# A recurrent attention layer and a top-2 expert layer on one core: the combination of expert outputs moved into the block loop

## The chip, the cores and the metric

The kernel runs on one core of one Trainium2 chip. The time is the device time of one execution in microseconds (us). Before the change it is 735.64 us, the median of three runs (734.95 to 736.15).

## The reference, cut to what matters

```python
# x: (2, 2048, 256)
x = layernorm(x + attn(x))       # token mixing, three 256x256 projections, an exponential
                                 # recurrence over T (wkv), a gate, an output projection
x = layernorm(x + ffn(x))
# ffn: 8 experts, 2 of them for each token
logits = x @ Wg + bg                                     # (tokens, 8)
topk_scores, topk_idx = top_k(logits, 2)
topk_scores = softmax(topk_scores)
comb = (one_hot(idx, 8) * topk_scores[..., None]).sum(axis=1)
h = einsum('td,edf->etf', tokens, W1) + b1[:, None, :]   # 256 -> 1024
a = where(even expert, gelu(h), silu(h))
y = einsum('etf,efd->etd', a, W2) + b2[:, None, :]       # 1024 -> 256
out = einsum('te,etd->td', comb, y)
# layernorm(z) = (z - mean) / sqrt(var + 1e-5)
```

## The kernel before, in words

All engines run programs of their own, and wait for each other by semaphores that are written out by hand. There are three stages.

The **chunk stage** walks over 8 chunks of 256 times 2 tokens (`chunks`, steps -2 to 9; a step works on several chunks at once). VectorE runs the scans of the recurrence (`stabilise`, `accumulate`, `numerator`, `divide`) and picks two experts for each token of an older chunk (`choose`, `place`). ScalarE runs, in each step and in this order, `exponents` (Relu and Exp, L1006 to L1011, whose result B is what `accumulate` multiplies at L1304), `bonuses` (Exp), `copy_x1T`, `gates` (Sigmoid), `upper_halves`, `inverse` (Ln and Exp), `normalise_x1` and `copy_v`. TensorE projects (`project_k` waits for VectorE's `nd`). GpSimd sends each token's normalised row, a record of 256 values and two numbers, to its two places in a table in DRAM, `records_dram`, sorted by expert (`send_records`, eight indirect DMAs a chunk); its spare time goes into splitting the weights of expert 0.

Every product of the experts is made from numbers that are split in an upper part (fp32r) and a lower part (the rest), in three products each. So weights and activations are split first.

The **block stage** works on blocks of 256 records of one expert. The count of blocks depends on the data, and tables made at its start (`row_t`, `ex_t`, `par_t`, `full_t`, VectorE's `link` chain) tell for each block where it lies, its expert, the slot of the weights and whether its second half holds anything. For a block t: ScalarE loads the records (`load_records`, three blocks ahead), TensorE transposes them (`turn_records`), VectorE splits the result (`halves`) and works out for each row where its output goes (`dest`, L1210), TensorE makes the first product (L897, 48 matmuls of 256 columns), ScalarE the function and the upper parts (L1102, L1108), VectorE the lower parts (L1220), TensorE the second product in two halves (L906, 24 matmuls each), VectorE adds the bias b2 (L1228, `outputs`), GpSimd scatters the rows to `expert_out_dram` with two indirect DMAs (L674). TensorE's order is: transposes of t+2, first product of t+1, second product of t. The code of TensorE is unrolled; VectorE, ScalarE and GpSimd run a loop with four blocks in its body (`blocks`). GpSimd also splits the weights of expert e (`split`, L580 and L584) when the blocks of expert e-2 are through; SP has loaded them as they are into one buffer (`staging`, 2 MB), one expert ahead. Two slots hold split weights (`wx`).

The **combination stage** begins when all rows have been written. SP loads for 16 pieces of 128 times 2 tokens the two expert rows of each token (`yy`; the rows x1 are there already), VectorE and ScalarE weigh them with the softmax scores and add x1, VectorE takes mean and variance, GpSimd a power of -0.5, ScalarE normalises, SP stores.

## Time and profile before

| | us |
|---|---|
| median of three runs | 735.64 |
| the profiled execution | 734.4 |
| its span, first to last instruction | 732.7 |
| TensorE busy | 643.3 (88%) |
| VectorE busy | 458.7 (63%) |
| ScalarE busy | 392.6 (54%) |
| GpSimd busy | 304.5 (42%) |
| TensorE in the chain that ended last | 72% |

In the profile PE is TensorE, PEld its weight loads, DVE VectorE, ACT ScalarE, POOL GpSimd and SP the sync engine. A name such as SPq is an engine's own instruction queue. L906 is line 906 of the kernel. Matmuls overlap, so their mean duration (283 ns) is more than the distance between two. The share of an engine over the span is a mean over three stages with different limits: the chunk stage lasts to about 250 us, the block stage to 672, the combination stage to the end. `[1.21 <-ACT ...]` behind an instruction is how long its engine stood idle ahead of it and what ended that.

### The profile page before, as it was taken

Reading aid. Unit: us, or ns where it says so; the run is one execution under the profiler, and the core shown is the slowest. Engines: PE = TensorE matmul, PEld = TensorE weight load, DVE = VectorE, ACT = ScalarE, POOL = GpSimd, SP = SyncE. Lnnn points to the kernel's source line nnn. Section 1 sums busy time; section 2 is a strip of 40 time slices with the busy share of each in tenths; the row PEclk is TensorE's granted clock in tenths of the full one; section 3 lists DMA queues with packets and bytes.
Section 4 is the critical chain, followed back from the end, with each engine's and each line's share of the span. In section 5 each row is a group of like instructions: output and inputs, shape, how many; then the busy total and the mean of one; then the engine's idle time right before and its main releaser. Section 6 shows DMA issues by size and latency. Waiting matters only on the chain.

```text
span 732.7 us, 14811 instructions
## 1 busy us (share of the span) xinstructions
PE 643.3 (88%) x4525; PEld 594.2 (81%) x4525; DVE 458.7 (63%) x963; ACT 392.6 (54%) x715; POOL 304.5 (42%) x353
## 2 busy tenths in 40 slices
PE   7999999999777889999999999999999999996000
PEld 4787877888655779999999999999999999996000
DVE  4879999999996465574654654455544543432694
ACT  3577577568742243654546363655645455551474
POOL 5111144654565636292361732551821821112363
PEclk9999999999987599999999999999999999999555
DMA  8400133132226517914141141141241121100893
GB/s 256 135 30 25 63 117 108 65 104 82 104 76 231 184 56 227 312 28 173 43 154 52 44 159 53 42 159 51 67 138 36 34 59 46 31 28 31 274 306 115
DMA packets 57116, 78.75 MB, mean 107 GB/s; under 512 B 5190, under 2 KB 46611, under 8 KB 56884
## 3 DMA queue, kind: packets, MB, share of 16 engines
q1 hardware_dynamic: 41540, 51.59, 21.8%
q0 software_dynamic: 6496, 16.99, 6.5%
q10 hardware_dynamic: 8976, 8.72, 4.4%
q8 instruction: 73, 1.20, 0.7%
q14 instruction: 31, 0.25, 0.1%
HBM read 49.14 MB, written 28.92 MB: 107 GB/s over the span
## 4 chain that ended last, share of the span: by engine, by line
PE 72%; DVE 10%; issue 7%; POOL 4%; ACT 3%; DMA 3%; SPq 0%; ACTq 0%; another core or an unknown queue 0%; DVEq 0%; POOLq 0%
PE hT_ps L897 28%; PE y_ps L906 26%; PE vr_ps L734 6%; PE k_ps L734 5%; PE xT_ps L915 2%; PE wo_ps L742 2%; POOL records_dram L639 2%; DVE o_all L1242 1%; PE xT_ps L725 1%; PE small_ps L756 1%; DMA yy<-expert_out_dram 1%; DMA recs<-records_dram 1%; POOL rstd_c L693 1%; PE xT_ps L804 1%; ACT res L1163 1%
## 5 line engine op out<-in xcount | busy, mean ns | idle before, releaser
L897 PE MATMUL hT_ps<-xTh,wx 128*128 128x256 f32 x1120 | 213.6, 288 | 3.8 <-DVE aTl L1220 2.6
L906 PE MATMUL y_ps<-wx,aTh 128*128 128x256 f32 x1088 | 197.5, 283 | 1.1 <-DVE y_sb L1228 1.1
L897 PEld LDWEIGHTS hT_ps<-xTh,wx 128*128 128x128 f32 x1120 | 179.9, 195 | 4.5 <-DVE aTl L1220 2.8
L1220 DVE TENSOR_TENSOR aTl<-hT_ps,aTh 128x512 fp32r<-128x512 f32 x140 | 93.1, 688 | 124.2 <-ACT aTh L1108 118.5
L906 PEld LDWEIGHTS y_ps<-wx,aTh 128*128 128x128 f32 x1088 | 169.7, 192 | 1.3 <-issue 1.3
L674 POOL DMA_INDIRECT expert_out_dram<-y_sb,dest x70 | 68.2, 975 | 238.3 <-DVE y_sb L1228 222.7
L897 PE MATMUL hT_ps<-xTl,wx 128*128 128x256 f32 x560 | 160.1, 286 | 0.0
L906 PE MATMUL y_ps<-wx,aTl 128*128 128x256 f32 x544 | 154.0, 283 | 0.0
L1102 ACT ACT_TABLE_LOAD x33 | 42.3, 1283 | 170.3 <-PE hT_ps L897 167.5
L1102 ACT ACTIVATE hT_ps<-hT_ps,b_c 128x256 f32<-128x256 f32 x280 | 113.3, 466 | 23.2 <-PE hT_ps L897 20.3
L897 PEld LDWEIGHTS hT_ps<-xTl,wx 128*128 128x128 f32 x560 | 109.1, 195 | 0.0
L906 PEld LDWEIGHTS y_ps<-wx,aTl 128*128 128x128 f32 x544 | 104.4, 192 | 0.0
L639 POOL DMA_INDIRECT records_dram<-rec,slot_i x64 | 75.3, 1177 | 65.8 <-DVE rec L1366 34.4
L734 PE MATMUL vr_ps<-xh,wq 128*128 128x512 f32 x256 | 86.6, 410 | 0.0
L1108 ACT ACTIVATE aTh<-hT_ps 128x512 fp32r<-128x512 f32 x140 | 83.8, 643 | 0.0
L1228 DVE TENSOR_TENSOR y_sb<-y_ps,b_b 128x256 f32<-128x256 f32 x70 | 29.4, 424 | 80.8 <-PE y_ps L906 79.0
L584 POOL TENSOR_TENSOR wx<-staging,wx 128x512 fp32r<-128x512 f32 x56 | 70.3, 1298 | 0.6
L734 PEld LDWEIGHTS vr_ps<-xh,wq 128*128 128x128 f32 x256 | 49.7, 194 | 11.8 <-ACT v L1001 0.3
L734 PE MATMUL vr_ps<-xl,wq 128*128 128x512 f32 x128 | 51.8, 405 | 0.0
L734 PE MATMUL k_ps<-xh,wq 128*128 128x512 f32 x128 | 42.2, 401 | 3.7 <-DVE nd L1249 2.7
L1210 DVE SCALAR_TENSOR_TENSOR dest<-recs,own_f 128x1 int32<-128x1 f32 x66 | 37.4, 607 | 0.1
L734 PEld LDWEIGHTS k_ps<-xh,wq 128*128 128x128 f32 x128 | 24.2, 189 | 10.3 <-issue 4.7
(201 smaller groups left out, 864.4 us busy)
## 6 DMA issues: line engine op xcount, KB each, us to landing
staging<-in_L_ffn_W SPq DMA_DIRECT2D x16, 1024.0 KB
recs<-records_dram ACTq DMA_DIRECT2D x33, 258.0 KB
yy<-expert_out_dram SPq DMA_DIRECT2D x16, 512.0 KB, 5.3
xin<-in_L_attn_x SPq DMA_DIRECT2D x16, 256.0 KB
xres<-in_L_attn_x SPq DMA_DIRECT2D x16, 256.0 KB, 3.1
x_dram<-rec SPq DMA_DIRECT2D x16, 256.0 KB
xx<-x_dram SPq DMA_DIRECT2D x2, 2048.0 KB
out<-res SPq DMA_DIRECT2D x16, 256.0 KB, 4.0
```

The costliest lines, as they stand in the source:

```text
L584: pool.tensor_tensor(wx[:, e % 2, 1, at], raw[:, at], wx[:, e % 2, 0, at].bitcast(F32), ALU.subtract).then_inc(weights_ready if n == LOWER ...
L639: pool.indirect_dma_start(xs, bass.IndirectOffsetOnAxis(ap=slot_i[at][:, n:n + 1], axis=0), rec[at][:, j, :], None, bounds_check=DUMMY - 1 ...
L674: pool.indirect_dma_start(ys, bass.IndirectOffsetOnAxis(ap=dest[t.slot][:, h:h + 1], axis=0), y_sb[t.slot][:, h, :], None, bounds_check=2 ...
L734: ins = pe.matmul(out_ps.rearrange("p (b t) -> p b t", b=B), wq[:, mat, now, part, cc, oc * P:(oc + 1) * P], xpart[c.slot][:, cc, :, now:n ...
L742: ins = pe.matmul(wo_bank(c, b)[:, h, :], mixed[:, cc, b, h * P:(h + 1) * P], wo[:, cc, :], start=cc == 0, stop=cc == CC - 1)
L897: ins = pe.matmul(hT_ps[b][:, f, :], wx[:, s, part, off:off + P], xpart[t.slot % 2][:, cc, :], start=k == 0, stop=k == len(terms) - 1)
L906: ins = pe.matmul(y_ps[h], apart[t.slot % 2][:, fc, h * P:(h + 1) * P], wx[:, s, part, off:off + C], start=k == 0, stop=k == len(terms) - 1)
L1102: act.activation(hT_ps[b][:, f, :], hT_ps[b][:, f, :], func, bias=b1_c[:, bass.ds(expert * FC + (2 * b + f), 1)]).then_inc(act_done, 1)
L1108: act.activation(aTh[u.slot % 2][:, 2 * b - 2:2 * b, :], hT_ps[b - 1][:], ACT.Copy).then_inc(aTh_done, 1)
L1210: dve.scalar_tensor_tensor(out=dest[u.slot][:, h:h + 1], in0=recs[u.slot][:, h, C + 1:REC], scalar=own[:, :, h:h + 1].rearrange("p a b -> ...
L1220: dve.tensor_tensor(aTl[u.slot % 2][:, 2 * b:2 * b + 2, :], hT_ps[b][:], aTh[u.slot % 2][:, 2 * b:2 * b + 2, :].bitcast(F32), ALU.subtract ...
L1228: dve.tensor_tensor(y_sb[u.slot][:, h, :], y_ps[h], b2_b[:, bass.ds(expert * C, C)], ALU.add).then_inc(y_done, 1)
```

## The change

The combination is done block by block. Since a layer norm doesn't change when its input is doubled and its epsilon multiplied by 4, the kernel works with 2z = (x1 + 2 g y) + (x1 + 2 g' y'), one bracket for each of a token's two experts. A record now holds 261 numbers: row, token, place of the first choice, the later one of its two places, and the two scores, which ScalarE makes in the chunk stage as sigmoids of the gap between the two logits (`weigh`). In the block stage:

- `mark`: eight small VectorE operations tell from the record whether this is the token's first or second visit, where it goes, and its weight.
- `share_half`: after the bias, a second VectorE operation makes x1 + 2 g y.
- GpSimd scatters the share to `x1_dram` where the visit is the token's first (`keep_shares`), gathers the earlier share for tokens on their second (`gather`), takes the power for the variances (`spread_z`) and scatters the finished rows to the output (`send_rows`): six indirect DMAs a block instead of two. Rows that are not concerned get an index out of bounds and are skipped.
- VectorE adds both shares and takes mean and variance (`add_other`, one block later), and normalises (`normalise`, two blocks later).

The combination stage, its loads and stores are gone. ScalarE no longer loads records; the sync engine does, and it fetches raw weights at the blocks that a new table names (`split_steps`, 13 operations once, at block 2). The split of weights leaves GpSimd: ScalarE writes the upper part in four pieces, VectorE the lower in four, behind `normalise`. The loops are unrolled on all engines. The core of the diff (declarations and the removed combination code left out):

```diff
-    LOWER = 8
+    SPLITS = 4
+    SECOND = EARLY + 1
+    MARKS = 8
     REGION = TOKENS + BLK
     DUMMY = E * REGION
-    REC = C + 2
+    REC = C + 5
...
+            def load_records(u):
+                row = sp.value_load(row_t[0:1, bass.ds(u.number, 1)], min_val=0, max_val=DUMMY)
+                sp.dma_start(recs[u.slot][:], xs[bass.ds(row, BLK), :].rearrange("(h p) c -> p h c", p=P)).then_inc(rec_in[u.slot], 16)
+
+            sp.wait_ge(pads_out, 16 * (E - 2))
+            for n in range(EARLY):
+                sp.wait_ge(share_done, early_block(n).upto(BH))
+                load_records(early_block(RING + n))
+            sp.wait_ge(weights_ready, 2)
+            load_raw(2)
+            sp.wait_ge(split_known, 1)
+
+            def block_step(t):
+
+                u = t + RING
+                if u.exists:
+                    with if_used(sp, used, u):
+                        sp.wait_ge(share_done, t.upto(BH))
+                        load_records(u)
+                fetch = sp.value_load(fetch_t[0:1, bass.ds(t.number, 1)], min_val=0, max_val=2)
+                with sp.If(fetch > 0):
+                    expert = sp.value_load(next_t[0:1, bass.ds(t.number, 1)], min_val=0, max_val=E - 3)
+                    sp.wait_ge(weights_ready, expert + 2)
+                    load_raw(expert + 2)
+
+            blocks_in_line(sp, used, 0, block_step)
...
+                          base=TC * c.number, channel_multiplier=1,
                           allow_small_or_imprecise_dtypes=True).then_inc(label_done, 1)
                 pool.wait_ge(label_done, c.upto(1))
+                pool.wait_ge(weighed, c.upto(2))
                 pool.wait_ge(x1_done, c.upto(J))
...
+            def spread_z(t):
+                pool.wait_ge(mv_z_done, since_second(t) * BH)
+                after(pool, row_done, since_second(t - RING) * BH)
+                pool.tensor_tensor(var_z[:], mv_z[t.slot][:, :, 1], eps4_b[:], ALU.add).then_inc(var_done, 1)
+                pool.wait_ge(var_done, since_second(t))
+                pool.tensor_tensor(rstd_z[t.slot][:], var_z[:], half_neg[:, 0:BH], ALU.pow).then_inc(rstd_z_done, 1)
+
+            def keep_shares(t):
+
+                pool.wait_ge(marks, t.upto(8))
+                pool.wait_ge(share_done, t.upto(BH))
+                take_wait(pool)
+                for h in range(BH):
+                    pool.indirect_dma_start(
+                        rows_1, bass.IndirectOffsetOnAxis(ap=where_to[t.number % MARKS][:, 0, h:h + 1], axis=0),
+                        share[t.slot][:, h, :], None, bounds_check=TOKENS - 1, oob_is_err=False).then_inc(share_out[t.slot], 16)
+
+            def gather(t):
+
+                pool.wait_ge(marks, t.upto(8))
+                pool.wait_ge(share_out[(t - 1).slot], (t - 1).turn(16 * BH, 16 * BH))
+                after(pool, sum_done, since_second(t - RING))
+                take_wait(pool)
+                for h in range(BH):
+                    pool.indirect_dma_start(
+                        other[t.slot][:, h, :], None, rows_1,
+                        bass.IndirectOffsetOnAxis(ap=where_to[t.number % MARKS][:, 1, h:h + 1], axis=0),
+                        bounds_check=TOKENS - 1, oob_is_err=False).then_inc(other_in[t.slot], 16)
+
+            def send_rows(t):
+                pool.wait_ge(row_done, since_second(t) * BH)
+                take_wait(pool)
+                for h in range(BH):
+                    pool.indirect_dma_start(
+                        rows_2, bass.IndirectOffsetOnAxis(ap=where_to[t.number % MARKS][:, 1, h:h + 1], axis=0),
+                        row_out[t.slot][:, h, :], None, bounds_check=TOKENS - 1, oob_is_err=False).then_inc(out_done[t.slot], 16)
+
+            keep_shares(early_block(0))
+
+            def block_step(t):
+                for stage, u in ((keep_shares, t - 1), (send_rows, t - 2), (gather, t), (spread_z, t - 1)):
+                    if stage is keep_shares:
+
+                        if t.exists:
+                            with if_used(pool, used, t, t.number - 1):
+                                stage(u)
+                    elif u.exists and with_second(u):
+                        with if_used(pool, used, u, t.number - 1):
+                            stage(u)
+
+            blocks_in_line(pool, used, 2, block_step)
...
+                pe.wait_ge(share_done, (t - 1).upto(BH, 1))
+                with pe.If(slot == 0):
+                    product2(t, 0, 0)
+                with pe.Else():
+                    product2(t, 1, 0)
+                pe.wait_ge(share_done, (t - 1).upto(BH))
+                with pe.If(full == 0):
+                    pe.sem_inc(mm2_done[1], 1)
+                with pe.Else():
...
+            def weigh(c):
+
+                at = c.number % RECS
+                act.wait_ge(gap_done, c.upto(1))
+                scattered(act, c)
+                act.activation(rec[at][:, :, C + 3], gap[:], ACT.Sigmoid, scale=-1.0).then_inc(weighed, 1)
+                act.activation(rec[at][:, :, C + 4], gap[:], ACT.Sigmoid).then_inc(weighed, 1)
...
+                if (i - 3).exists and i.number < NCH:
+                    weigh(i - 3)
                 if i.exists:
...
+                if i.number == NCH:
+                    weigh(i - 2)
                 if (i - 1).exists:
                     normalise_x1(i - 1)
+                if i.number in (NCH - 1, NCH + 1):
+                    weigh(i - 2)
                 if (i + 1).exists and i.number >= 0:
...
+            def split_upper(t):
+
+
+                kind = act.value_load(split_t[0:1, bass.ds(t.number, 1)], min_val=0, max_val=2)
+                with act.If(kind > 0):
+                    expert = act.value_load(next_t[0:1, bass.ds(t.number, 1)], min_val=0, max_val=E - 1)
+                    slot = act.value_load(opp_t[0:1, bass.ds(t.number, 1)], min_val=0, max_val=1)
+                    for h in range(BH):
+                        act.wait_ge(mm2_done[h], kind + (t.number - 1))
+                    act.wait_ge(raw_in, expert * 32 + 64)
+                    take_wait(act)
+                    for n in range(SPLITS):
+                        at = bass.ds(n * WE // SPLITS, WE // SPLITS)
+                        act.activation(wx[:, bass.ds(slot, 1), 0, at].rearrange("p a b -> p (a b)"), raw[:, at], ACT.Copy).then_inc(hi_done, 1)
...
+                if t.number == EARLY:
+                    act.wait_ge(split_known, 1)
+                split_upper(t)
+
+            blocks_in_line(act, used, 0, block_step)
...
+            def mark(u, own):
+
+
+                n = u.slot % 2
+                rows = recs[u.slot]
+                dve.tensor_tensor(is_top[n][:], rows[:, :, C + 1], own, ALU.is_equal).then_inc(marks, 1)
+                dve.tensor_tensor(is_late[n][:], rows[:, :, C + 2], own, ALU.is_equal).then_inc(marks, 1)
+                dve.tensor_tensor(is_early[n][:], rows[:, :, C + 2], own, ALU.not_equal).then_inc(marks, 1)
+                dve.tensor_tensor(lead[n][:], rows[:, :, C + 3], rows[:, :, C + 4], ALU.subtract).then_inc(marks, 1)
+                if u.number >= MARKS:
+                    old = u - MARKS
+                    dve.wait_ge(share_out[old.slot], old.turn(16 * BH, 16 * BH))
+                    if with_second(old):
+                        dve.wait_ge(out_done[old.slot], in_ring(old) * 16 * BH)
+                dve.wait_ge(marks, u.upto(8, 2))
+                dve.scalar_tensor_tensor(out=where_to[u.number % MARKS][:, 0, :], in0=is_late[n][:], scalar=float(NOWHERE),
+                                         in1=rows[:, :, C], op0=ALU.mult, op1=ALU.add).then_inc(marks, 1)
+                dve.wait_ge(marks, u.upto(8, 3))
+                dve.scalar_tensor_tensor(out=where_to[u.number % MARKS][:, 1, :], in0=is_early[n][:], scalar=float(NOWHERE),
+                                         in1=rows[:, :, C], op0=ALU.mult, op1=ALU.add).then_inc(marks, 1)
+                dve.wait_ge(marks, u.upto(8, 4))
+                dve.scalar_tensor_tensor(out=twice[n][:], in0=is_top[n][:], scalar=2.0, in1=lead[n][:],
+                                         op0=ALU.mult, op1=ALU.mult).then_inc(marks, 1)
+                dve.wait_ge(marks, u.upto(8, 7))
+                dve.scalar_tensor_tensor(out=weight[u.slot][:], in0=rows[:, :, C + 4], scalar=2.0, in1=twice[n][:],
+                                         op0=ALU.mult, op1=ALU.add).then_inc(marks, 1)
...
+            def share_half(u, h, expert):
+
+                if h == 0:
+                    after(dve, share_out[u.slot], u.turn(16 * BH))
+                    after(dve, sum_done, since_second(u - RING))
+                    dve.wait_ge(marks, u.upto(8))
+                dve.wait_ge(mm2_done[h], u.upto(1))
+                dve.tensor_tensor(y_ps[h], y_ps[h], b2_b[:, bass.ds(expert * C, C)], ALU.add).then_inc(y_done, 1)
+                dve.wait_ge(y_done, u.upto(BH, h + 1))
+                dve.scalar_tensor_tensor(out=share[u.slot][:, h, :], in0=y_ps[h], scalar=weight[u.slot][:, h:h + 1],
+                                         in1=recs[u.slot][:, h, 0:C], op0=ALU.mult, op1=ALU.add).then_inc(share_done, 1)
+
+            def shares(u):
+                expert = dve.value_load(ex_t[0:1, bass.ds(u.number, 1)], min_val=0, max_val=E - 1)
                 for h in range(BH):
-                    dve.wait_ge(mm2_done[h], u.upto(1))
-                    dve.tensor_tensor(y_sb[u.slot][:, h, :], y_ps[h], b2_b[:, bass.ds(expert * C, C)],
-                                      ALU.add).then_inc(y_done, 1)
+                    share_half(u, h, expert)
+
+            def add_other(u):
+                dve.wait_ge(other_in[u.slot], in_ring(u) * 16 * BH)
+                after(dve, out_done[u.slot], (in_ring(u) - 1) * 16 * BH)
+                dve.wait_ge(share_done, u.upto(BH))
+                dve.tensor_tensor(row_out[u.slot][:], share[u.slot][:], other[u.slot][:], ALU.add).then_inc(sum_done, 1)
+                dve.wait_ge(sum_done, since_second(u))
+                for h in range(BH):
+                    dve.bn_stats(stats_z[u.slot][:, h, :], row_out[u.slot][:, h, :]).then_inc(bn_z, 1)
+                dve.wait_ge(bn_z, since_second(u) * BH)
+                take_wait(dve)
+                for h in range(BH):
+                    dve.bn_aggr(mv_z[u.slot][:, h, :], stats_z[u.slot][:, h, :]).then_inc(mv_z_done, 1)
+
+            def normalise(u):
+                dve.wait_ge(rstd_z_done, since_second(u))
...
+                dve.tensor_tensor(rec[c.number % RECS][:, :, C + 2], slot_f[:, :, 0], slot_f[:, :, 1], ALU.max).then_inc(slots, 1)
...
+            def split_steps():
+
+
+                some = lambda a: a[:, 1:E - 1].unsqueeze(1).broadcast_to([P, BLOCKS, E - 2])
+                link(dve.tensor_scalar(short_f[:], blocks_f[:], 2.0, -2.0, ALU.min, ALU.add))
+                link(dve.tensor_tensor(place_f[:], starts_f[:], short_f[:], ALU.add))
+                link(dve.tensor_scalar(kind_f[:], short_f[:], -1.0, 1.0, ALU.mult, ALU.add))
+                link(dve.tensor_tensor(past_e[:, :, 0:E - 2], block_f[:, :, 1:E - 1], some(place_f), ALU.is_equal))
...
+            def split_lower(t):
+
+                kind = dve.value_load(split_t[0:1, bass.ds(t.number, 1)], min_val=0, max_val=2)
+                with dve.If(kind > 0):
+                    expert = dve.value_load(next_t[0:1, bass.ds(t.number, 1)], min_val=0, max_val=E - 1)
+                    slot = dve.value_load(opp_t[0:1, bass.ds(t.number, 1)], min_val=0, max_val=1)
+                    for n in range(SPLITS):
+                        at = bass.ds(n * WE // SPLITS, WE // SPLITS)
+                        dve.wait_ge(hi_done, expert * SPLITS + (n + 1))
+                        take_wait(dve)
+                        flat = lambda part: wx[:, bass.ds(slot, 1), part, at].rearrange("p a b -> p (a b)")
+                        dve.tensor_tensor(flat(1), raw[:, at], flat(0).bitcast(F32),
+                                          ALU.subtract).then_inc(weights_ready if n == SPLITS - 1 else lower_done, 1)
...
                 if u.exists:
-                    with if_used(dve, used, u):
-                        halves(u, own_f[:, bass.ds(u.number, 1)])
+                    with if_used(dve, used, u, known):
+                        halves(u)
+                        mark(u, own_f[:, u.number, :])
+                u = t - 2
+                if u.exists and with_second(u):
+                    with if_used(dve, used, u, known):
+                        normalise(u)
+                if t.number > EARLY and (t - 1).exists:
+                    split_lower(t - 1)
                 u = t + 1
                 if u.exists:
-                    with if_used(dve, used, u):
+                    with if_used(dve, used, u, known):
...
+                u = t - 1
+                if u.exists and with_second(u):
+                    with if_used(dve, used, u, known):
+                        add_other(u)
+                if t.exists:
+                    with if_used(dve, used, t, known):
+                        shares(t)
+                        if t.number == EARLY:
+                            split_steps()
+                            dve.wait_ge(split_known, 1)
+
+            blocks_in_line(dve, used, 2, block_step)
```

## Rows read from the trace of the kernel before

**Rows 1.** Busy time of the engines in one stretch, granted clock, share of DMA.
```profile
320.00:660.00 340.00, 339.70 (x2844) 339.46 (x2843) 166.60 (x286) 180.71 (x376) 133.23 (x110) 1.00 0.24 75
```
**Rows 2.** The chain that ended last, in order of time: start, duration, what.
```profile
366.12 5.76 PE y_ps L906 x48
372.31 5.75 PE hT_ps L897 x48
...
666.05 6.03 PE y_ps L906 x48
673.40 3.27 DMA expert_out_dram<-y_sb,dest
```
**Rows 3.** Timeline (start, duration, engine, line) of early records, a block, and the end.
```profile
237.14 0.34 DVE L1210 SCALAR_TENSOR_TENSOR dest<-recs,own_early 128x1 int32<-128x1 f32 x2
...
372.35 0.69 DVE L1204 CAST xTh<-xT_ps 128x512 fp32r<-128x512 f32 x1
379.71 1.29 DVE L1220 TENSOR_TENSOR aTl<-hT_ps,aTh 128x512 fp32r<-128x512 f32 x2 [0.56 <-ACT aTh L1108]
...
662.26 0.42 DVE L1228 TENSOR_TENSOR y_sb<-y_ps,b_b 128x256 f32<-128x256 f32 x1 [0.20 <-PE y_ps L906]
663.56 0.97 POOL L674 DMA_INDIRECT expert_out_dram<-y_sb,dest  x1 [7.85 <-DVE y_sb L1228]
...
687.63 0.74 DVE L1512 BATCH_NORM_STATS2 stats_c<-zz 128x6 f32<-128x256 f32 x2
...
724.35 0.69 POOL L693 TENSOR_TENSOR rstd_c<-var_e,half_neg 128x2 f32<-128x2 f32 x1
```
**Rows 4.** Timeline of ScalarE in the block whose step starts at 371.87.
```profile
373.86 1.28 ACT L1102 ACT_TABLE_LOAD   x1 [5.69 <-PE hT_ps L897]
```
**Rows 5.** A page group, a line of the splits, the timeline while one runs.
```profile
L1220 DVE TENSOR_TENSOR aTl<-hT_ps,aTh 128x512 fp32r<-128x512 f32 x140 | 93.1, 688 | 124.2 <-ACT aTh L1108 118.5
...
L580 POOL TENSOR_SCALAR wx<-staging x7: 3612/3632/3652, 271.4 to 572.1; 128x4096 fp32r<-128x4096 f32 x7
...
361.85 4.19 DVE L1210 SCALAR_TENSOR_TENSOR dest<-recs,own_f 128x1 int32<-128x1 f32 x2
```
**Rows 6.** Timeline of ScalarE and VectorE in the chunk stage, steps 4, 5 and 7.
```profile
114.51 0.21 ACT L1036 ACTIVATE xh<-xh 128x4 fp32r<-128x4 f32 x1 [4.93 <-PE xT_ps L725]
...
119.78 1.38 DVE L1249 SCALAR_TENSOR_TENSOR nd<-o_all,consts_c,k_ps 128x512 f32<-128x512 f32 x2
...
125.16 1.04 ACT L1009 ACTIVATE B<-B 128x1024 f32<-128x1024 f32 x1
126.24 1.23 DVE L1304 TENSOR_TENSOR b2v<-B,v 128x1024 f32<-128x1024 f32 x1
...
140.46 0.21 ACT L1036 ACTIVATE xh<-xh 128x4 fp32r<-128x4 f32 x1 [5.09 <-PE xT_ps L725]
141.66 1.28 ACT L1045 ACT_TABLE_LOAD   x1
142.95 1.06 ACT L1045 ACTIVATE r<-den 128x1024 f32<-128x1024 f32 x1
145.72 1.38 DVE L1249 SCALAR_TENSOR_TENSOR nd<-o_all,consts_c,k_ps 128x512 f32<-128x512 f32 x2
...
193.67 2.08 ACT L1054 ACTIVATE rec<-xres,shift,rstd 128x256 f32<-128x256 f32 x4 [1.19 <-POOL shift L619]
```
**Rows 7.** Timeline: an indirect DMA's issue beside scans, and a stop of VectorE.
```profile
207.16 1.88 POOL L639 DMA_INDIRECT records_dram<-rec,slot_i  x1 [0.30 <-issue]
...
232.29 0.39 DVE L1278 MAX8 m<-small_ps 128x8 f32<-128x8 f32 x4 [2.25 <-remote]
```
**Rows 8.** The last stores, and landing times of loads and stores (page, last number).
```profile
724.99 1.85 SPq L524 DMA_DIRECT2D out<-res  x2
...
yy<-expert_out_dram SPq DMA_DIRECT2D x16, 512.0 KB, 5.3
out<-res SPq DMA_DIRECT2D x16, 256.0 KB, 4.0
```

370 lines of the change are left out of this document (121 added, 249 removed).

## The prediction

> **What bounds the kernel now.** I read the windows first: from 320 to 660 us TensorE is busy all the time at a granted clock of 1.00 (its upper level, 2.4 GHz), while VectorE is busy half and GpSimd 39% of it [rows 1]. The chain of waits says the same in order of time: in the block stage it is nothing but TensorE, 5.76 us for a second product, 5.75 for a first, and 0.43 between them for four transposes, so a block costs 11.95 us with no gap [rows 2]. There are 140 / 4 = 35 blocks [rows 5]. The last second product ends at 672.1; the rest, 60.6 us, is the combination stage [rows 2]. Before the blocks the chunk stage has a period of 25.95 us (nd at 119.78 and at 145.72 [rows 6]), in which VectorE, TensorE and ScalarE are all close to the bound; it matters here, because the change puts work on ScalarE there.
>
> **The change part by part.** All in the profiled execution's own time: span 732.7, 734.4 with what lies around it, and the median of the runs is 735.64, 1.24 above that.
>
> *The tail.* It goes (60.6 us) and a drain of two pipeline steps replaces it. In the last step but one VectorE has the lower parts of block 34, then the sum of block 32, then the shares of 33. In before, TensorE started the last second product at 666.05 [rows 2], 1.4 after the one ahead of it had ended, since it waited for the bias sum of block 33; now it waits only for the first half's share, some 0.85 us earlier, so it ends at 671.0. From there (old time base): shares of 33 are done at 666.0; GpSimd wakes 0.9 later (y_sb ends at 662.68, its DMA starts at 663.56) and issues one indirect DMA each 1.28 (0.97 [rows 3] plus a gap of 0.30 [rows 7]), keep_shares(33) at 666.9 to 669.2, send_rows(32) to 671.7, gather(34) 672.0 to 674.3, spread_z(33) to 675.4, send_rows(33) after its normalisation, 677.0 to 679.2. The gathered rows land 3.3 after their second issue, at 676.6 (the one indirect DMA on the chain took 3.27 [rows 2]; a gather isn't in the trace, the nearest are 3.27 and the 5.3 of the yy load of 512 KB [rows 8], and I take 3.3 for the same 128 rows of 1 KB). The sum of block 34 is 0.7 (xTh has its size), the two statistics 0.75, the aggregates 0.25 (small ones like dest, 0.17 and less each, and a wait) [rows 3]: 678.6, hidden behind GpSimd, whose power (0.7) comes at 679.3 to 680.3. Normalisation 0.8 (two at no more than the 0.42 of y_sb, which has its size), send_rows(34) 682.1 to 684.4, landed at 686.7. In before the last result was issued at about 726.6 and landed 4.0 later [rows 8], and the span ended 2.1 behind that: span end 688.8. The part gives 732.7 - 688.8 = **-43.9**; with a gather of 5.3 instead of 3.3, -42.
>
> *The block stage.* VectorE gets more work. One block, in order: second half of the shares 0.9 (bias sum 0.42, then a scalar_tensor_tensor, taken as the same 0.42), halves 1.4 [rows 3], the eight marks 1.1 (two dest took 0.34 [rows 3], so 8 x 0.17 = 1.4 at most and half of it if independent ones overlap; I take 1.1, nearer the row), normalisation 0.8, an If and its loads 0.6, lower parts 4 x 0.65, sum and statistics 1.85, first half of the shares 0.9: 10.2 us of 11.95. The lower parts are paced by ScalarE; the last two begin at 379.71 behind its aTh and end at 381.00, 9.1 after the step's start at 371.88 [rows 2, 3]. With 1.85 and 1.8 behind them VectorE is 1.0 into the next step, which is where it stands in before (y_sb is the first thing there). TensorE needs these results one product later, so nothing waits. ScalarE was busy 180.7 of 340 us [rows 1] and stands still for 5.7 us before each block [rows 4]; the four upper splits are 4 x 1.05 = 4.2 (the 128x1024 rows [rows 6]) and fit in. The four lower ones on VectorE are 4 x 1.23 = 4.9 [rows 6]: in that step the lower parts end 12.3 in, the first of them at 10.4, needed at 12.4; the lag is 3.1 and 1.9 of it goes in each following step. Seven splits lie between 271.4 and 572.1, 50.1 us or 4.2 blocks apart in the mean [rows 5], and the next expert's first product comes four blocks after its split starts, so weights aren't late. Raw weights are now asked for when the split ahead is through, one block into an expert, three blocks or 36 us before they are wanted. GpSimd loses its splits and gets 0.9 + 6 x 1.28 + 1.2 = 9.8 of 11.95 per block. Its port conflict goes too: two dest of 0.17 took 4.19 while its operation of 3.63 us ran [rows 5], but that was hidden. Block stage: **0**, with 0.3 for the entry, where halves of block 3 come behind the first split (283.9 instead of 282.5) and the first lower part of block 2 ends when TensorE wants its bank.
>
> SP now issues record loads behind share_done, pads and split_known (13 table steps, about 3.8 us after the shares of block 2); ScalarE waits for these too and starts block 4 some 3 us late, ending 11.6 into a step where 12.4 is the limit. Hidden; without that cover 3 us once.
>
> *The chunk stage.* ScalarE gets weigh(): two sigmoids of 128x4 (0.21 each [rows 6]), and they stand between copy_v and the exponents, where the loaded table is that of Exp. So the pair costs a load of the sigmoid table, and before the next Exp a load back: 2 x 1.29 + 0.44 = 3.0 us in steps 3 to 7. A switch costs 1.29: the load starts at 141.66, with no idle time before it, and Ln at 142.95 [rows 6]. Is it covered? ScalarE's B is ready at 126.20 and VectorE takes it (b2v) at 126.24, just as its own earlier work ends: no cover at all [rows 6]. The loop it lengthens spans two steps: b2v to the end of nd 20.9 (126.24 to 147.10), nd to xh through TensorE 19.3 (121.16 to 140.46), xh to B ready 11.7 (114.51 to 126.20) [rows 6]; 51.9 = 2 x 25.95. With 3.0 more it is 54.9, 1.5 a step. The first step pays 3.0 at once. Step by step b2v is late by 3.0, 3.8, 6.1, 6.8 and 6.9 (in step 7 ScalarE has slack, 1.2 of it before rec [rows 6]). The last indirect writes and the early blocks hang on that: **+6.9**. If the shared loop doesn't soften it, it is 5 x 3.0 = 15; if the reload is hidden, near 0. The third slot column and the placing of weigh among the last chunks add 0.3.
>
> The page ScalarE: Activation LUTs (What ACT_TABLE_LOAD costs) of the Trainium skill gives a load 1.28 us and adds a drain of 1.38. The trace agrees with the load and shows no such drain, the next function starting 1.29 after the load's start; with the page's price weigh would cost 5.8 instead of 3.0, and the part would be some 13 instead of 6.9, the total 705.
>
> **Sum.** -43.9 + 0.3 + 6.9 + 0.3 = -36.4. 734.4 - 36.4 = 698.0, and on the scale of the median 735.6 - 36.4 = **699.2 us**.
>
> **The rivals.**
> 1. *VectorE becomes the bound.* My sum of 10.2, plus 4.9 / 4.3 for the splits, is 11.3 of 11.95. Its code is now unrolled with Ifs that are jumped over, and near the end of the chunk stage it stood still for 2.25 us for something the profile can't name ("remote") [rows 7]. If marks or such a stop add 1.2 a block, the step is 12.5: 33 x 0.55 = 18, so 717. Against it: TensorE's code is unrolled with Ifs already, without a gap.
> 2. *GpSimd's descriptors are starved; slower than before.* An indirect DMA's issue took 1.88 instead of 0.97 while VectorE ran its scans [rows 7]. If all six were so, GpSimd's step is 0.9 + 6 x 2.18 + 1.2 = 15.2, 3.2 over the period, and its lag ends in share buffers of which there are four: 33 x 3.2 = 106 on top, 805. It decides from 13.1 a block (1.83 a DMA with its gap). Against it: VectorE's operations on SBUF alone in a block are 1.3 us plus marks, outside split steps.
> 3. *The chunk stage pays in full*, 15 instead of 6.9: 707. For it: b2v and what stands around it follow without idle time [rows 6]. Against: half of the loop is TensorE and ScalarE.
> 4. *The sigmoids cost nothing*, because the table serves both, or the period is VectorE's own: 692. For it: VectorE's own earlier work ends when B does.
>
> For rival 2 the page SBUF — State Buffer (SBUF: two separate sides) of the Trainium skill says that a DMA whose descriptors GpSimd writes waits whenever VectorE holds the shared port. The trace shows such stretching once scans run, and in the block stage 0.97 nearly everywhere; how much of the new VectorE work takes the port no row here shows.
>
> **How the numbers follow.** Forecast 0.57 (own range 692 to 707), rival 1 0.14, rival 2 0.06, rival 3 0.12, rival 4 0.11. A measurement of this kernel tells 0.2% (1.5 us) from no change. Faster by more than that: all but rival 2 and a little of 1, 0.92; within 0.2% 0.02; slower 0.06. The range reaches from 689, below rival 4 by a shorter drain, to 717, rival 1.
>
> **What would show it.** Right: the second products still 11.95 apart; nothing but two or three pipeline steps (15 to 20 us) behind the last; the o_all scans of steps 4 to 7 27 to 28 us apart, and b2v released by B of ScalarE; two table loads more in each of those steps. Wrong: gaps of TensorE released by share_done or aTl at each block (rival 1), indirect issues near 1.9 (rival 2), first products released by the lower weights.

## The result: slower, and the profile after

The changed kernel takes 746.84 us (median of 5 runs, 741.12 to 749.54) where the kernel before takes 734.95 beside it: ratio 1.0163, 95% interval 1.0135 to 1.0191. I had forecast 699.2. The profiled execution is the fastest of the five, 741.12 us with a span of 739.4.

The windows of the same stretch as in [rows 1], for the changed kernel. Columns: stretch, length, then busy time and instructions of TensorE, its weight loads, VectorE, ScalarE, GpSimd; granted clock, share of DMA, GB/s.
```profile
320.00:660.00 340.00, 317.34 (x2570) 308.86 (x2569) 251.57 (x673) 197.60 (x373) 187.18 (x204) 0.98 0.27 81
```
In [rows 1] TensorE got 2844 matmuls into this stretch at a clock of 1.00; now it gets 2570 in. 9.6% of 340 us, 33 us, are gone, and at most 7 of them to the clock (2% of 340). The chain of waits shows how they go (start, duration, what):
```profile
338.35 5.60 PE y_ps L906 x48
344.39 5.68 PE hT_ps L897 x48
...
363.08 4.41 PE y_ps L906 x36
...
429.73 3.85 PE y_ps L906 x33
```
A first and a second product undisturbed are 5.68 and 5.60, and the first blocks follow each other every 11.7 us, even a little faster than in [rows 2]. But from 367 us on products break off after 33 or 36 of their 48 matmuls. What TensorE waited for from 297 us to the end (us, times, longest):
```profile
PE y_ps L906 <- issue: 12.7, 26, 1.1
PE hT_ps L897 <- issue: 8.3, 13, 1.1
PE hT_ps L897 <- DVE aTl L1235: 2.9, 2, 1.5
```
"issue" means that nothing which the profile knows held it. Before, this list has one wait of 0.3 us for issue in that stretch. ScalarE stops too (us, times, longest; "remote" is a release by something that the profile can't name):
```profile
ACT hT_ps L1110 <- remote: 23.8, 12, 2.6
ACT L1110 <- remote: 23.4, 3, 7.9
ACT L1110 <- issue: 13.3, 3, 7.8
```
The first row is the one that matters: idle time between ScalarE's functions in the middle of a block, of which the kernel before has none with this releaser. The other two are the wait ahead of a block's table load, which before has as well (5.7 us a block, [rows 4]); here it has grown to 7.9 in places.

By stage, in the profiled executions: the last nd ends at 206.05 instead of 197.66 (+8.4, of which 6.1 are left when the first second product starts); the blocks, from that start to the end of the last second product, take 445.2 us (274.8 to 720.0) instead of 403.3 (268.8 to 672.1), +41.9; and the span ends 19.4 behind the last product instead of 60.6, -41.2. 6.1 + 41.9 - 41.2 = 6.8, the 6.7 between the spans. The tail gave nearly what was forecast, and the block stage took it all back. Of its 41.9 us, TensorE's stops inside a product are 25.2; gaps at the edges of products, for issue or for VectorE's lower parts, are about 10 more, and matmuls that follow each other a little less closely about 6.

### The profile page after: what moved, and what is told of

It reads as the page before. It is cut to its first block, busy times and chain, and to the rows that moved or that the text cites. A ratio compares the mean times of both kernels' runs of the same rounds, so it can differ in the third digit from the quotient of the medians.

```text
span 739.4 us, 14979 instructions
## 1 busy us (share of the span) xinstructions
PE 656.4 (89%) x4525; PEld 597.7 (81%) x4525; DVE 546.9 (74%) x1399; ACT 414.1 (56%) x709; POOL 355.8 (48%) x422
## 3 DMA queue, kind: packets, MB, share of 16 engines
q0 software_dynamic: 12544, 21.34, 8.7%
## 4 chain that ended last, share of the span: by engine, by line
PE 62%; DVE 12%; issue 12%; ACT 8%; POOL 2%; DMA 1%; DVEq 1%; another core or an unknown queue 1%; ACTq 0%; SPq 0%; POOLq 0%
PE hT_ps L897 24%; PE y_ps L906 23%; PE vr_ps L734 5%; PE k_ps L734 4%; PE xT_ps L915 2%; PE wo_ps L742 1%; PE small_ps L756 1%; ACT rec L1059 1%; DVE aTl L1235 1%; DVE o_all L1290 1%; POOL records_dram L619 1%; ACT hT_ps L1110 1%; DVE stats L1388 1%; ACT L1027 1%
## 5 line engine op out<-in xcount | busy, mean ns | idle before, releaser
L906 PE MATMUL y_ps<-wx,aTh 128*128 128x256 f32 x1088 | 201.1, 285 | 12.4 <-issue 10.7
L1235 DVE TENSOR_TENSOR aTl<-hT_ps,aTh 128x512 fp32r<-128x512 f32 x140 | 90.1, 686 | 69.5 <-ACT aTh L1116 48.4
L1110 ACT ACTIVATE hT_ps<-hT_ps,b_c 128x256 f32<-128x256 f32 x280 | 112.7, 461 | 50.1 <-remote 23.8
L660 POOL DMA_INDIRECT x_dram<-share,where_to x68 | 70.3, 1035 | 106.0 <-issue 95.1
L619 POOL DMA_INDIRECT records_dram<-rec,slot_i x64 | 78.1, 1220 | 66.3 <-DVE rec L1415 34.9
L671 POOL DMA_INDIRECT other<-x_dram,where_to x64 | 70.8, 1107 | 31.5 <-issue 31.5
L680 POOL DMA_INDIRECT out<-row_out,where_to x64 | 65.3, 1021 | 24.5 <-issue 19.5
L1250 DVE TENSOR_TENSOR y_ps<-y_ps,b_b 128x256 f32<-128x256 f32 x70 | 30.0, 429 | 37.6 <-issue 18.8
L734 PE MATMUL k_ps<-xh,wq 128*128 128x512 f32 x128 | 45.3, 427 | 8.5 <-DVE nd L1297 7.7
L734 PEld LDWEIGHTS k_ps<-xh,wq 128*128 128x128 f32 x128 | 26.1, 204 | 16.0 <-issue 9.6
```

Of the source, the lines that this page charges most:

```text
L619: pool.indirect_dma_start(xs, bass.IndirectOffsetOnAxis(ap=slot_i[at][:, n:n + 1], axis=0), rec[at][:, j, :], None, bounds_check=DUMMY - 1 ...
L660: pool.indirect_dma_start(rows_1, bass.IndirectOffsetOnAxis(ap=where_to[t.number % MARKS][:, 0, h:h + 1], axis=0), share[t.slot][:, h, :], ...
L671: pool.indirect_dma_start(other[t.slot][:, h, :], None, rows_1, bass.IndirectOffsetOnAxis(ap=where_to[t.number % MARKS][:, 1, h:h + 1], ax ...
L680: pool.indirect_dma_start(rows_2, bass.IndirectOffsetOnAxis(ap=where_to[t.number % MARKS][:, 1, h:h + 1], axis=0), row_out[t.slot][:, h, : ...
L734: ins = pe.matmul(out_ps.rearrange("p (b t) -> p b t", b=B), wq[:, mat, now, part, cc, oc * P:(oc + 1) * P], xpart[c.slot][:, cc, :, now:n ...
L906: ins = pe.matmul(y_ps[h], apart[t.slot % 2][:, fc, h * P:(h + 1) * P], wx[:, s, part, off:off + C], start=k == 0, stop=k == len(terms) - 1)
```

## The experiments

The question was what stops TensorE, VectorE and ScalarE in the middle of straight code. Where a time is given, the ratio to the kernel before, run on the same chip, follows with its interval. "Burst" is how many indirect transfers GpSimd issues in a row, at most 0.8 us between the end of one and the start of the next. "TensorE stops" are its gaps inside a product that the profile puts down to issue, added up from the trace: what the starts of two matmuls are apart beyond the usual 0.12 us, where that is 0.2 us or more, from 297 us to the end of the last product. "ScalarE stops" are its waits in the middle of a block that end with "remote" (hT_ps <- remote, from 297 us on). The expectations count otherwise: their stops of TensorE take in gaps of up to 1.6 us at the edges of products, whatever ended them, and end at 700 us (66.5 for b_more4, 5.7 for a_spread). "Block stage" is as above. Before's time is its median on each chip, 734.2 to 735.4.

| run | transfers a block | burst | time, us | ratio (95%) | block stage, us | TensorE stops, us | ScalarE stops, us |
|---|---|---|---|---|---|---|---|
| before | 2 | 1 or 2 | 734.9 | | 403.3 | 0 | 0 |
| b_more2 | 4 | 4, some of 6 and 8 | 749.2 | 1.021 (1.017 to 1.024) | 418.9 | 11.7 | 6.2 |
| b_more4 | 6 | 6, some of 12 | 827.1 | 1.127 (1.122 to 1.133) | 494.6 | 70.3 | 96.8 |
| after | 6 | 6, at first 2 | 746.8 | 1.016 (1.014 to 1.019) | 445.2 | 25.2 | 23.8 |
| a_no_rows | 6, no rows moved | 6 | 747.5 | 1.018 (1.013 to 1.022) | 449.5 | 30.3 | 31.1 |
| a_half_rows | 6 of 64 rows | 6 | 754.8 | 1.029 (1.026 to 1.032) | 453.1 | 35.1 | 31.1 |
| a_scatter_instead | 6 | 6 | 758.3 | 1.031 (1.028 to 1.034) | 454.2 | 36.2 | 26.7 |
| a_order_only | 6 | 6 | 773.2 | 1.051 (1.047 to 1.056) | 471.0 | 55.2 | 88.9 |
| a_no_gather | 4 | 4 | 704.5 | 0.958 (0.953 to 0.963) | 407.0 | 1.9 | 11.6 |
| a_plain_copy | 4 and 2 plain | 4 | 696.3 | 0.949 (0.946 to 0.951) | 403.3 | 0.2 | 10.1 |
| a_only_gather | 2 | 2 | 691.7 | 0.940 (0.939 to 0.942) | 400.9 | 0 | 0 |
| a_spread | 6, two pauses | 4 and 2 | 722.2 | 0.985 (0.981 to 0.989) | 420.4 | 0.2 | 31.9 |
| a_even | 6, two pauses | 2 | 707.2 | 0.962 (0.960 to 0.964) | 403.7 | 0 | 0 |

**First theory: instruction fetch.** The changed kernel writes out the block loops of ScalarE and VectorE, and the rows of instruction packets seemed to fit: q14 went from 31 to 65 packets. Four runs together. b_unrolled writes the loops out in the kernel before:
```diff
-            blocks(act, block_step)
+            blocks_unrolled(block_step)      # for n in range(EARLY, BLOCKS + 1): body(Step(None, n, ...))
...
-            blocks(dve, block_step)
+            blocks_unrolled(block_step)
```


> The kernel before, with nothing changed but that ScalarE's and VectorE's block loops are written out instead of running as a loop of four blocks (ScalarE 1054 to 2163 instructions, VectorE 631 to 765); the work done is the same. Fetch theory (the changed kernel's block stage lost about 40 us because the written-out code of ScalarE, VectorE, GpSimd and SyncE has to be fetched all through the stage, beside TensorE's own): q14 brings instruction packets all through the block stage, TensorE stops in mid-product with nothing to wait for, and the time rises by 10 to 40 us, to 745 to 775. Row-traffic theory (the six indirect transfers of each block delay everything): no change, 735 within 2 us. Engine-work theory (VectorE's and ScalarE's added work is the bound): no change, 735 within 2 us.

Measured 734.47 us, ratio 0.9991 (0.9978 to 1.0004): nothing, though q14 has half as many packets again and ScalarE twice the code. Its page (packets, MB, share):
```profile
q14 instruction: 45, 0.37, 0.2%
```
The reverse on the changed kernel, ScalarE's loop alone, and all four engines':
```diff
-            blocks_in_line(act, used, 0, block_step)
+            blocks_rolled(act, used, block_step)     # eng.Fori over four blocks, as before
```


> The changed kernel with ScalarE's block code alone as a loop of four blocks again (2735 to 1268 instructions), its work the same, the others written out. Fetch theory: ScalarE's idle time in mid-branch, put down to remote and issue, goes (about 60 us of it in all now), and with it half or more of TensorE's 28.7 us of stops in mid-product: 741 to 705 to 725 us. Row-traffic theory and engine-work theory: no change, 741 to 747 us.

> The changed kernel with ScalarE's and SyncE's block code as loops of four blocks and VectorE's and GpSimd's as loops of eight (SyncE 647 to 335 instructions, VectorE 2087 to 1601); the work is the same. Fetch theory: the block stage of 37 blocks comes back to its pace before the change, 11.7 to 11.9 us a block, and 35 to 42 us go: 700 to 708 us. If a loop of eight is too long to stay resident, VectorE is still fetched: 710 to 725. Row-traffic theory and engine-work theory: no change, 741 to 747 us.

Measured 751.4 (ratio 1.020, 1.015 to 1.025) and 760.3 (1.033, 1.028 to 1.038), where written out it is 1.016: nothing comes back. The theory falls.

**Second theory: the rows' traffic.** All row indices out of bounds (`ALU.mult` to `ALU.max` in the two where_to lines), the instructions kept:

> The changed kernel with every row index of the block stage out of bounds, so that its six indirect transfers per block are issued but move no row (the combination's rows and the output are left out). Row-traffic theory: the block stage loses its 40 us, time about 700 us, and TensorE's stops in mid-product go. Fetch theory: instruction code is the same, so the stops stay: 738 to 747 us, save 1 to 2 us at the end where the last rows don't travel. Engine-work theory: as the fetch theory.

747.5 us (1.018, 1.013 to 1.022), with q0 down from 21.34 to 8.80 MB. It isn't the bytes. But laying TensorE's gaps beside GpSimd's instructions gave the lead: of the time in the gathers of L671 22% falls into such a gap, of that in L660 and L680 0 to 1%. GpSimd in such a block of the changed kernel:
```profile
350.88 1.05 POOL L660 DMA_INDIRECT x_dram<-share,where_to  x1 [2.25 <-issue]
352.24 1.02 POOL L660 DMA_INDIRECT x_dram<-share,where_to  x1 [0.31 <-issue]
353.61 0.97 POOL L680 DMA_INDIRECT out<-row_out,where_to  x1 [0.34 <-issue]
354.88 0.97 POOL L680 DMA_INDIRECT out<-row_out,where_to  x1 [0.30 <-issue]
356.51 1.05 POOL L671 DMA_INDIRECT other<-x_dram,where_to  x1 [0.65 <-issue]
357.86 1.01 POOL L671 DMA_INDIRECT other<-x_dram,where_to  x1 [0.30 <-issue]
```
The gathers are also the fifth and sixth transfer in a row. So: the gather itself, or the burst, or what VectorE does at that place? Three runs that leave rows out, so what they write isn't the reference's result:
```diff
# a_no_gather (the same with share_out and out_done in a_only_gather)
-                    pool.indirect_dma_start(other[t.slot][:, h, :], None, rows_1, ...).then_inc(other_in[t.slot], 16)
+                pool.sem_inc(other_in[t.slot], 16 * BH)
# a_scatter_instead
+                    pool.indirect_dma_start(rows_3, ...where_to[...][:, 1, h:h + 1]..., other[t.slot][:, h, :], None, ...)
```


> The changed kernel without the two indirect gathers of a block (the earlier choice's rows are not fetched; its buffer stays zero), the four indirect scatters and all work of VectorE and ScalarE kept. TensorE's stops in mid-product fall in the traces on GpSimd's gathers and the 1 to 2 us behind them (22% of L671's time, 0 to 1% of L660's and L680's). Gather theory (issuing a gather stops the other engines): the stops go, and 28 to 40 us with them, 747 to 705 to 718 us. Burst theory (the fifth and sixth indirect transfer in a row do it): the same here. Place theory (it is VectorE's added adds and statistics, which run at that time): the stops stay, 740 to 747 us.

> The changed kernel with only the two gathers of a block left of its six indirect transfers (the four scatters replaced by the semaphore increments of their completion, so neither shares nor output rows are written). Gather theory: the stops stay, 25 to 40 us of them, 738 to 750 us. Burst theory: no burst of six, so they go: 705 to 718 us. Place theory: they stay.

> The changed kernel with each of the two gathers replaced by a scatter of the same buffer by the same indices to a scratch tensor: six indirect transfers a block, none of them a gather (the earlier choice's rows are not fetched). Gather theory: the stops go, 705 to 718 us. Burst theory: they stay, 740 to 750 us. Place theory: they stay, 740 to 750 us.

Without gathers 704.5, with nothing but gathers 691.7, with scatters in their place 758.3; the last two lie 13 and 8 us outside what was expected, on the side that the burst theory points to. That leaves the burst: a gather stops nothing that a scatter doesn't, and VectorE's added work, which is in all three, costs nothing where the burst is gone (block stage 400.9).

**What counts, and is it enough alone?** b_more4 puts the burst into the kernel before, with no other part of the change; a_half_rows halves its descriptors; a_plain_copy sends as many rows by a plain queue (other rows than the reference's); a_spread pulls the burst apart.
```diff
# b_more4 (MORE = 2; b_more2 has MORE = 1), behind each scatter of y_sb
+                        for n in range(MORE):
+                            pool.indirect_dma_start(more[n], ...dest[t.slot][:, h:h + 1]..., y_sb[t.slot][:, h, :], None, ...)
# a_spread
-   ((keep_shares, t - 1), (send_rows, t - 2), (gather, t), (spread_z, t - 1)):
+   ((keep_shares, t - 1), (send_rows, t - 2), (spread_z, t - 1), (gather, t)):
+       if stage in (send_rows, gather):
+           pool.tensor_tensor(paused[:], eps4_b[:], half_neg[:, 0:BH], ALU.pow)
```


> The kernel before, with each of the two indirect scatters of a block issued three times (the two copies go to scratch tensors by the same rows): six indirect transfers a block, no other work of the change. Backlog theory (TensorE, VectorE and ScalarE are stopped once about five of GpSimd's indirect transfers fall in 8 us, whatever they carry; in the changed kernel there are no stops at 0 to 3 in the last 8 us, 20 in 96 us at five and 22 in 24 us at six): the block stage, unchanged otherwise, gets the same stops, 25 to 45 us, and the time is 760 to 780. Interplay theory (it needs VectorE's added instructions too): under 10 us of stops, 735 to 745.

> The changed kernel with each of its six indirect transfers of a block cut from 128 to 64 rows (the other half of the rows is neither kept, fetched nor sent). Backlog of rows (what piles up is one descriptor or packet per row): three transfers' worth of rows, the stops go, 700 to 710 us. Backlog of instructions (what counts is GpSimd's six instructions of 1 us each): the stops stay, 735 to 750 us.

> The changed kernel with GpSimd's two gathers of a block replaced by two plain copies of 128 rows of 1 KB issued by SyncE one block ahead (other data than the reference's, same rows and bytes). If what piles up is traffic or packets of any queue: as the changed kernel, 740 to 750. If it is GpSimd's indirect transfers alone: as without the gathers, 700 to 710.

> The changed kernel with GpSimd's six indirect transfers of a block kept but spread over it: the spread of the norm moved between the output rows and the gather, and one dummy power of two elements (about 0.7 us, no traffic) ahead of the output rows and one ahead of the gather. Backlog theory: hardly a window of 8 us with six, mostly four (3 stops in 106 us in the changed kernel): stops fall to 10 to 15 us and the time to 715 to 728. If only the mean rate counts (six in 11.7 us): no change, 740 to 750.

b_more4: 827 us, 93 us on top of a kernel to which nothing was added but 140 instructions of 0.97 us on an engine with idle time. More than I expected. TensorE and GpSimd in one of its bursts (timeline: start, duration, engine, line, what, idle time before):
```profile
389.04 10.05 POOL L586 TENSOR_TENSOR wx<-staging,wx 128x512 fp32r<-128x512 f32 x8
399.23 1.01 POOL L676 DMA_INDIRECT expert_out_dram<-y_sb,dest  x1
...
409.50 0.97 POOL L680 DMA_INDIRECT more_dram<-y_sb,dest  x1 [0.30 <-issue]
409.87 0.28 PE L912 MATMUL y_ps<-wx,aTh 128*128 128x256 f32 x1 [0.34 <-issue]
...
410.77 0.97 POOL L676 DMA_INDIRECT expert_out_dram<-y_sb,dest  x1 [0.30 <-issue]
...
411.99 0.28 PE L912 MATMUL y_ps<-wx,aTh 128*128 128x256 f32 x1 [0.91 <-issue]
412.05 0.97 POOL L680 DMA_INDIRECT more_dram<-y_sb,dest  x1 [0.31 <-issue]
413.33 0.97 POOL L680 DMA_INDIRECT more_dram<-y_sb,dest  x1 [0.30 <-issue]
413.39 0.37 PE L912 MATMUL y_ps<-wx,aTl 128*128 128x256 f32 x1 [1.12 <-issue]
```
From the seventh transfer on the two go in step: while transfers follow each other 1.28 us apart, TensorE gets at most three matmuls through for each, where eleven would fit (5.60 us are 48). This burst is not of six but of twelve: GpSimd has just split weights for 13.7 us, the six transfers of one block have waited for that, and those of the next follow without a break. The one at 399.23 is the first of the twelve, the one at 409.50 the ninth. The stretch of windows for this run:
```profile
320.00:660.00 340.00, 299.64 (x2295) 288.84 (x2294) 127.96 (x235) 152.09 (x311) 215.20 (x192) 0.94 0.31 99
```
Half the rows save nothing (754.8, with q0 at 9408 packets where the changed kernel has 12544): it is the instructions, not rows, bytes or descriptors. Two plain copies of the same size on SyncE's queue cost nothing (696.3, the block stage at before's 403.3). Pulled apart, the six cost less (722.2), but not nothing: the block stage is still 17 us longer than before's, though TensorE's products hardly stop (0.2 us). ScalarE stops instead, VectorE's lower parts wait for it, and TensorE for them (a_spread, us, times, longest):
```profile
ACT hT_ps L1123 <- remote: 31.9, 15, 3.0
PE hT_ps L910 <- DVE aTl L1248: 6.7, 5, 1.8
```
a_spread breaks its six into a burst of four and one of two, and nearly all of these stops end within 0.9 us behind the fourth transfer of a four. Such stops need not cost time: a_plain_copy has 10.1 us of them at no loss in its block stage.

**How do the stops grow, and can all six be had for nothing?** b_more2 is the step between. a_even moves the two dummy powers of a_spread so that one stands ahead of the kept shares and one ahead of the output rows; the spread of the norm is the third break.

> The kernel before, with each of the two indirect scatters of a block issued twice: four a block in one burst of some 5.2 us, no other work of the change. Two a block gave no stops, six a block 66.5 us of them and 93 us in all. Backlog theory: in the changed kernel and in the run with six, stops begin at four in 8 us (3 in 106 us, 7 in 57 us) and are frequent from five; four a block reach five in 8 us hardly ever, so stops are few: 5 to 15 us, 740 to 752. If the loss went with the plain number of transfers (93 us for 148 added ones), half of it: 780.

> The changed kernel with all six transfers of a block and the same two dummy powers as in a_spread, which then stand ahead of the kept shares and ahead of the output rows, so that no four transfers follow each other without a pause (in a_spread two gathers and two kept shares do, and 11 stops of 5.7 us were left, 3.7 us of them in the send of the output rows behind them). If density counts: fewer stops than in a_spread, 715 to 722 us. If the mean rate counts: as a_spread, 722 within 3.

b_more2: 749.2, a seventh of the price of b_more4 for half the added transfers. a_even: 707.2, faster than either theory had it, and no stop. What TensorE's stops go with is the length of the burst, in each of these traces:

| run | bursts | TensorE's stops |
|---|---|---|
| b_more2 | 20 of four | none |
| b_more2 | 6 of six or eight | 16, 9.8 us |
| b_more4 | 20 of six | 39, 24.5 us |
| b_more4 | 6 of twelve | 62, 45.8 us |
| after | 17 of two or four | none |
| after | 23 of six | 40, 24.2 us |
| a_order_only | 29 of six | 74, 54.8 us |
| a_no_gather | 29 of four | 7, 1.9 us |
| a_even | 92 of two | none |

In the changed kernel all but one of the stops come at the fifth or sixth transfer of a burst. Its first blocks, up to 350 us, have bursts of two, with one of four, and no stop; b_more2's stops come where a split of weights has driven the transfers of two blocks together. So b_more4 does not suffer much more than the changed kernel from a burst of six (1.2 us against 1.1); the rest of the difference is its bursts of twelve, 7.6 us each. A burst of six costs 1.9 us in a_order_only, and why it does isn't shown. GpSimd in a_even:
```profile
408.20 0.73 POOL L663 TENSOR_TENSOR paused<-eps_b,half_neg 128x2 f32<-128x2 f32 x1
409.13 1.11 POOL L671 DMA_INDIRECT x_dram<-share,where_to  x1 [0.20 <-issue]
410.55 1.00 POOL L671 DMA_INDIRECT x_dram<-share,where_to  x1 [0.31 <-issue]
411.55 0.74 POOL L663 TENSOR_TENSOR paused<-eps_b,half_neg 128x2 f32<-128x2 f32 x1
412.48 1.03 POOL L691 DMA_INDIRECT out<-row_out,where_to  x1 [0.19 <-issue]
413.82 0.99 POOL L691 DMA_INDIRECT out<-row_out,where_to  x1 [0.30 <-issue]
414.82 0.22 POOL L652 TENSOR_TENSOR var_z<-mv_z,eps_b 128x2 f32<-128x2 f32 x1
415.12 0.71 POOL L654 TENSOR_TENSOR rstd_z<-var_z,half_neg 128x2 f32<-128x2 f32 x1
```
A pause of a microsecond after each pair, on an engine that had the time, and these windows:
```profile
320.00:660.00 340.00, 339.75 (x2842) 339.33 (x2840) 276.05 (x748) 215.46 (x410) 255.81 (x283) 1.00 0.28 86
```
2842 matmuls where [rows 1] has 2844. a_even changes the order as well, so the last pair of runs takes its two parts asunder and tries to mend its end:

> The changed kernel with GpSimd's order of a_even (kept shares, output rows, spread of the norm, gather) and no dummy powers. Density theory: the gathers of a block are followed by the kept shares and the output rows without a pause, still six in a row of 8 us, so the stops stay: 735 to 750 us. If the order took them away: 705 to 712.

> a_even up to block 33, and from block 34 on the changed kernel's own order without dummy powers. Behind the last product a_even has 15.3 us to the end of the last row's normalisation and the changed kernel 10.5: if the pauses and the late gather are the difference, 3 to 5 us go, less 1 to 2 us for stops that may come back in the last four blocks: 703 to 706 us. If not, 707.

The order without the pauses is slower than the changed kernel itself and than both answers expected, 773.2: gathers, kept shares and output rows in one burst of six, and 43% of the time in the last of them (L680 there) falls into a gap of TensorE. The pauses do it. a_even_tail: 706.5 (0.960, 0.957 to 0.963), not to be told from a_even; pauses and stops weren't what its end was longer by, and I leave the 5 us there open. Both are faster than either kernel of the case, with all of the computation.

**The chunk stage.** weigh(i - 3) moved behind gates(i + 1), where the sigmoid table is loaded already:
```diff
-                if (i - 3).exists and i.number < NCH:
-                    weigh(i - 3)
                 if i.exists:
                     exponents(i)
...
                     gates(i + 1)
+                if (i - 3).exists and i.number < NCH:
+                    weigh(i - 3)
```


> The changed kernel with ScalarE's two sigmoids of the routing weights (L1027, L1028) moved from the head of the chunk step to right behind the gates' sigmoid, in steps 3 to 15: same instructions, but two table loads of 1.28 us fewer a step. Table theory (the chunk stage lost 8.4 us because the two table loads stand ahead of the exponentials, on the chain from nd to k_ps): 6 to 9 us faster than the changed kernel, 738 to 741 us on this chip. If the loss there had come from another addition to the step (VectorE's two copies of slots, GpSimd's records), no change, 745 to 749.

773.6 us (1.050, 1.046 to 1.055): both answers wrong. The first such step is cured: nd follows nd by 25.8 us (93.85, 119.64) where the changed kernel has 28.8 (93.92, 122.74). But the next takes 32.0:
```profile
119.64 1.38 DVE L1297 SCALAR_TENSOR_TENSOR nd<-o_all,consts_c,k_ps 128x512 f32<-128x512 f32 x2
...
151.64 1.38 DVE L1297 SCALAR_TENSOR_TENSOR nd<-o_all,consts_c,k_ps 128x512 f32<-128x512 f32 x2
```
In that step TensorE waits 2.0 us for xres (wo_ps, from 135 us on), and then runs at a lower granted clock (0.50 is its lower level, 1.2 GHz):
```profile
133.00:149.00 16.00, 13.99 (x53) 11.50 (x52) 14.45 (x36) 6.30 (x12) 9.52 (x8) 0.68 0.18 64
...
141.00:145.00 4.00, 4.00 (x20) 4.00 (x20) 3.57 (x15) 0.00 (x0) 3.09 (x4) 0.50 0.28 100
```
Idle time and clock together are some 7 us (2.0, and 0.32 of 16), enough for the 6 that the step lost. That the idle moment brought the clock down is not shown: in the kernel before it falls too, to 0.70 from 137 to 141 us, with TensorE busy throughout. And most of the loss is elsewhere. At the last nd the two runs are 2.2 us apart (206.86 against 204.66), at the first second product 13.4 (288.18 against 274.82); what makes the 11.2 us between I haven't found. The rest is in the blocks, 463.2 us with 42.0 of TensorE's stops: the same six transfers a block cost more than in the changed kernel, and why isn't shown.

## Why the prediction was wrong

The step that failed is the block stage, "Block stage: **0**". I added up each engine's work by its busy time and found room on all of them: VectorE 10.2 of 11.95, ScalarE, and "GpSimd loses its splits and gets 0.9 + 6 x 1.28 + 1.2 = 9.8 of 11.95 per block". As an account of work these sums were good enough: in a_even VectorE is busy 276.1 of 340 us, 9.7 us a block with the splits, where I had 11.3, and with the work of the change in place and the burst broken up the block stage takes 403.7 us against 403.3. What the sum has no line for is that indirect transfers issued back to back, six in a burst, stop *other* engines. +41.9 us, of which a_even gives back 41.5, and b_more4 shows the cost without the rest of the change.

- *The tail*, -43.9: measured -41.2, by the steps named. 1.1 of the forecast was an earlier end of the last product, and behind that product I had 17.8 us where 19.4 were measured. The end of the changed kernel (timeline):
```profile
719.74 0.28 PE L906 MATMUL y_ps<-wx,aTl 128*128 128x256 f32 x1
...
723.11 1.15 POOL L680 DMA_INDIRECT out<-row_out,where_to  x1 [2.48 <-DVE row_out L1276]
724.57 0.99 POOL L680 DMA_INDIRECT out<-row_out,where_to  x1 [0.31 <-issue]
...
726.63 0.73 DVE L1276 TENSOR_SCALAR row_out<-row_out,mv_z,rstd_z 128x256 f32<-128x256 f32 x2 [2.09 <-POOL rstd_z L652]
728.25 1.04 POOL L680 DMA_INDIRECT out<-row_out,where_to  x1 [1.66 <-DVE row_out L1276]
729.60 0.97 POOL L680 DMA_INDIRECT out<-row_out,where_to  x1 [0.30 <-issue]
```
- *The chunk stage*, +6.9 and 0.3: measured +8.4. The mechanism is there, two table loads of 1.28 us around the sigmoids; sigmoids, load and load back are 2.8 us where I had 3.0 (97.50 to 99.00, and 1.29 from 101.01 on):
```profile
97.50 1.28 ACT L1027 ACT_TABLE_LOAD   x1
98.79 0.21 ACT L1027 ACTIVATE rec<-gap 128x4 f32<-128x4 f32 x1
98.90 0.19 ACT L1028 ACTIVATE rec<-gap 128x4 f32<-128x4 f32 x1
99.00 1.05 ACT L1003 ACTIVATE B<-nd 128x1024 f32<-128x1024 f32 x1
99.95 1.04 ACT L1004 ACTIVATE A<-nd 128x1024 f32<-128x1024 f32 x1
101.01 1.28 ACT L1006 ACT_TABLE_LOAD   x1
```
  The next function starts 1.29 us after each load's start, as in [rows 6]; the drain of 1.38 us that the Trainium skill adds (ScalarE: Activation LUTs, What ACT_TABLE_LOAD costs) is not there in either kernel. The steps were 28.8, 26.9, 28.5 and 26.5 us long; the shared loop softened it by about half, as I had it: nd is late by 3.0, 3.9, 6.5 and 8.4 us, step by step. a_weigh_late shows that taking the loads out of that place doesn't give the time back.
- *Rival 2*, the only one that ended slower, had GpSimd as the place and the wrong victim: it starves itself, at 1.88 us an issue. The issues took 1.02 to 1.11 us on average:
```profile
L671 POOL DMA_INDIRECT other<-x_dram,where_to x60 | 66.7, 1112 | 30.3 <-issue 30.3
L680 POOL DMA_INDIRECT out<-row_out,where_to x56 | 57.3, 1023 | 18.5 <-issue 17.6 <-DMA x_dram<-share,where_to 0.9
```
  The Trainium skill's rule (SBUF — State Buffer, SBUF: two separate sides) that GpSimd's descriptors wait for VectorE's hold of the port therefore cost next to nothing here.
- *Rival 1* had the sign that mattered: engines standing still for "remote". I had the row of it, 2.25 us of VectorE up to 232.29 [rows 7]. I took it for instruction fetch, priced it for VectorE alone, and argued it away with TensorE's gapless code. What stands beside it in the kernel before is the end of a burst of eight indirect transfers, the first at 221.98, and the stop ends as the last of them does:
```profile
231.30 0.97 POOL L639 DMA_INDIRECT records_dram<-rec,slot_i  x1 [0.30 <-issue]
```
  That these transfers caused the stop is not shown for the chunk stage, but this was the row that would have warned me.

Left open: what the engines share with GpSimd's indirect issue. The trace has no row for it. Plain queues, bytes, rows, instruction loops and VectorE's load are excluded, and so is GpSimd being busy for long as such: before's seven splits keep it busy for 13.7 us each, and no product of TensorE breaks off for issue. The number of transfers in a burst counts. Kernels that have only bursts of two lose nothing, bursts of four stop ScalarE (a_spread, a_no_gather, a_plain_copy; hardly in b_more2) and TensorE next to not at all, bursts of six stop both. What a break has to be, idle time or work, and how long, no run here tells apart: a_even's pairs stand 0.9 us apart, and in b_more2 three stops of 1.9 us fall beside a pair that comes 1.2 us behind a burst of six.
